# Softmax denominators and row maxima turned by fewer TensorE passes, and new hand-written orders on every engine

## The reference, cut to what matters

```python
x_norm = group_norm(x, gn1_gamma, gn1_beta, GROUPS).reshape(b, c, n)
qkv = jnp.einsum('oc,bcn->bon', qkv_w, x_norm) + qkv_b[None, :, None]
...
attn = jnp.einsum('bhnd,bhmd->bhnm', q, k) / math.sqrt(head_dim)
attn = jax.nn.softmax(attn, axis=-1)
x_attn = jnp.einsum('bhnm,bhmd->bhnd', attn, v)
...
x_attn = jnp.einsum('oc,bcn->bon', out_w, x_attn) + out_b[None, :, None]
x_attn = group_norm(x_attn, gn2_gamma, gn2_beta, GROUPS)
...
x_attn = jax.nn.silu(h1) * gate
x_attn = x_attn @ mlp2_w.T
...
return x + x_attn
```

## Time and profile before

| | us |
|---|---|
| median of 3 runs | 162.49 (162.44 to 163.28) |
| the profiled execution, its own time | 163.85 |
| span of the profiled execution | 162.1 |
| PE busy | 153.3 |
| DVE busy | 100.2 |
| ACT busy | 89.6 |
| POOL busy | 58.0 |

### The profile page before, as it was taken

One profiled execution on the slowest core, in us unless ns is written; L12 is line 12 of the kernel. 1 busy time (PEld: TensorE's weight loads), 2 busy tenths in 40 slices (PEclk: granted clock), 3 DMA queues, 4 the chain that ended last, 5 costly groups with the idle time before them and its releaser, 6 DMA issues.

```text
span 162.1 us, 3214 instructions
## 1 busy us (share of the span) xinstructions
PE 153.3 (95%) x1160; PEld 125.0 (77%) x1160; DVE 100.2 (62%) x223; ACT 89.6 (55%) x160; POOL 58.0 (36%) x107
## 2 busy tenths in 40 slices
PE   7699999999799997999999999999999999999993
PEld 5245786699477776798697999689699698799991
DVE  0750585547999864798487788776947155254331
ACT  8859764523217577576566872345675477424120
POOL 7079985580002075040670000490000671704400
PEclk9999999999999999999999999999999999999999
DMA  3999100424360070600702424100000000001010
GB/s 95 247 395 343 47 4 0 117 77 131 100 165 0 2 194 9 184 11 6 189 8 76 126 70 128 35 2 2 6 0 34 32 4 0 32 0 36 0 65 32
DMA packets 11407, 12.17 MB, mean 75 GB/s; under 512 B 1456, under 2 KB 9584, under 8 KB 11392
## 3 DMA queue, kind: packets, MB, share of 16 engines
q1 hardware_dynamic: 11360, 11.94, 25.3%
q0 software_dynamic: 32, 0.04, 0.3%
HBM read 4.56 MB, written 1.05 MB: 35 GB/s over the span
## 4 chain that ended last, share of the span: by engine, by line
PE 78%; DMA 7%; DVE 6%; SPq 4%; issue 2%; POOL 1%; ACT 1%; DVEq 0%; ACTq 0%; POOLq 0%
PE ps L754 9%; PE po L778 9%; PE pm L728 9%; PE px L849 7%; PE ps L664 5%; SPq L288 4%; PE po L804 4%; PE po L790 3%; PE pm L691 3%; PE pf L664 3%; PE pf L650 3%; DMA k_stack<-qk_parts 3%; PE pf L651 3%; PE pf L652 3%; DVE neg_max L1407 3%; DMA fac<-in_factors 2%
## 5 line engine op out<-in xcount | busy, mean ns | idle before, releaser
L1407 DVE TENSOR_REDUCE neg_max<-pm 128x2 f32<-128x512 f32 x64 | 42.3, 685 | 12.7 <-PE pm L728 12.4
L474 ACT ACTIVATE up_t<-ps 128x512 f32<-128x512 f32 x64 | 36.1, 593 | 16.0 <-PE ps L754 8.6
L728 PE MATMUL pm<-k_stack,q_stack 127*128 127x256 f32 x128 | 28.5, 308 | 2.2 <-DMA k_stack<-qk_parts 1.1
L754 PE MATMUL ps<-q_stack,k_stack 128*128 128x256 f32 x128 | 27.1, 305 | 0.5 <-ACT up_t L474 0.2
L728 PEld LDWEIGHTS pm<-k_stack,q_stack 127*128 127x128 f32 x128 | 19.6, 189 | 7.0 <-issue 2.3
L754 PEld LDWEIGHTS ps<-q_stack,k_stack 128*128 128x128 f32 x128 | 19.4, 189 | 3.5 <-issue 1.2
L359 POOL TENSOR_TENSOR sq<-gs 128x2 f32<-128x2 f32 (+1 forms) x5 | 1.0, 193 | 53.0 <-DVE gs L1362 53.0
L778 PE MATMUL po<-up_t,v_aug 128*32 128x256 f32 x256 | 16.7, 384 | 0.3 <-DVE gs L1362 0.3
L849 PE MATMUL px<-win,w_s 128*128 128x256 f32 x56 | 15.5, 387 | 0.0
L650 PE MATMUL pf<-xm_hi,w_hi 128*128 128x256 f32 x44 | 13.9, 315 | 0.0
L652 PE MATMUL pf<-xm_hi,w_lo 128*128 128x256 f32 x44 | 12.4, 281 | 0.0
(11 more groups left out here) (117 smaller groups left out, 319.3 us busy)
## 6 DMA issues: line engine op xcount, KB each, us to landing
win<-in_xw SPq DMA_DIRECT2D x12, 256.0 KB, 6.7
q_stack<-qk_parts SPq DMA_DIRECT2D x24, 128.0 KB, 2.4
k_stack<-qk_parts SPq DMA_DIRECT2D x24, 128.0 KB, 2.7
out<-win SPq DMA_DIRECT2D x8, 128.0 KB, 1.7
w_s<-in_w SPq DMA_DIRECT2D x1, 512.0 KB, 5.4
w_s<-in_w SPq DMA_DIRECT2D x1, 256.0 KB, 5.9
wqk_s<-in_wqk SPq DMA_DIRECT2D x1, 128.0 KB, 5.5
wo_s<-in_wo SPq DMA_DIRECT2D x1, 128.0 KB, 4.8
```

The costliest lines, as they stand in the source:

```text
L474: act.activation(probs[:, h // HALF, h % HALF, :, :].rearrange("p c n -> p (c n)"), ps[:, h % 2, :], ACT.Exp, scale=D ** -0.5).then_inc(pr ...
L728: return pe.matmul(pm[:, h % 2, c * N:(c + 1) * N], stack_rows(q_stack, i, slice(0, TOP))[:, h, c * 128:(c + 1) * 128], stack_rows(k_stack ...
L754: return pe.matmul(ps[:, h % 2, c * N:(c + 1) * N], stack_rows(k_stack, i, slice(0, TOP + 1))[:, h, c * 128:(c + 1) * 128], stack_rows(q_s ...
L1407: dve.tensor_reduce(neg_max[:, i % 2, :, h], pm[:, h % 2, :].rearrange("p (c n) -> p c n", c=2), AX.X, ALU.max, negate=True).then_inc(max_ ...
```

## The change

`turn_sums` becomes four transposes of whole 128x128 blocks of `sums`, and `invert` reads the 16 denominators of a pixel out of these blocks with a strided pattern. `neg_max` becomes 128 wide for each image, blank but for 16 columns, so that `turn_maxima` is one transpose of a 128x128 tile; ACT reads 16 x 128 in place of 8 x 256, and the DMA of `rows` has 16 pieces for 8. One memset on DVE blanks `neg_max` at the start. And the lists of calls of SP, POOL, ACT, PE and DVE are put in new orders.

```diff
-        neg_max = sb("neg_max", [128, 2, 2, HEADS])
-        max_row = sb("max_row", [HEADS, N], F32R)
+        neg_max = sb("neg_max", [128, 2, 128])
+        max_row = sb("max_row", [2 * HEADS, 128], F32R)
...
-            for j in range(0, 3):
-                stack(j)
+            stack(0)
+            stack(1)
             rows(0)
+            stack(2)
             rows(1)
             stack(3)
...
             stack(5)
+            stack(6)
             rows(4)
-            stack(6)
-            stack(7)
             rows(5)
             store(0)
+            stack(7)
+            store(1)
             rows(6)
             rows(7)
...
-                act.activation(max_row[:, :], pm[0:HEADS, 1, 0:N], ACT.Copy).then_inc(rows_read, 1)
+                act.activation(max_row[:, :], pm[0:2 * HEADS, 1, 0:128], ACT.Copy).then_inc(rows_read, 1)
...
             def turn_maxima(i):
                 pe.wait_ge(max_read, HEADS * (i + 1))
-                for c in range(2):
-                    mm = pe.transpose(pm[0:HEADS, 1, c * 128:(c + 1) * 128], neg_max[:, i % 2, c, :], ident_s[:, :])
-                mm.then_inc(turn_done, 1)
+                if i < 2:
+                    pe.wait_ge(blank_ready, 1)
+                pe.transpose(pm[:, 1, 0:128], neg_max[:, i % 2, :], ident_s[:, :]).then_inc(turn_done, 1)
...
                 for c in range(2):
                     for half in range(2):
-                        a = c * HEADS + half
-                        mm = pe.matmul(po[:, 0, a:a + HEADS - 1:2], sums[:, half, c * 128:(c + 1) * 128],
-                                       ident_s[:, D - D * half::32], start=True, stop=True)
+                        a = (2 * c + half) * 128
+                        mm = pe.transpose(po[:, 0, a:a + 128], sums[:, half, c * 128:(c + 1) * 128], ident_s[:, :])
                 mm.then_inc(den_done, 1)
...
+            dve.memset(neg_max[:, :, :], 0.0).then_inc(blank_ready, 1)
...
-                dve.reciprocal(inv[:, :, :].rearrange("p c h -> p (c h)"), po[:, 0, 0:2 * HEADS]).then_inc(inv_ready, 1)
+                dens = po[:, 0, D:D + 1]
+                dve.reciprocal(inv[:, :, :].rearrange("p c (g u) -> p c u g", u=2),
+                               bass.AP(tensor=dens.tensor, offset=dens.offset, ap=[dens.ap[0], (2 * 128, 2), (128 - D, 2), (32, HALF)])).then_inc(inv_ready, 1)
```

More of the change, by code:

```diff
@@ L887, in _ @@
             maxima(0, 3, 1)
-            downsample(7)
             project_v(1)
@@ L927, in _ @@
+            scores(0, 5, 0)
+            scores(0, 5, 1)
+            maxima(1, 7, 0)
+            maxima(1, 7, 1)
+            weigh(0, 0, 0)
+            weigh(0, 0, 1)
+            scores(0, 6, 0)
+            scores(0, 6, 1)
+            scores(0, 7, 0)
+            scores(0, 7, 1)
             maxima(2, 0, 0)
             maxima(2, 0, 1)
-            scores(0, 4, 0)
-            scores(0, 4, 1)
+            project_qk(3)
             turn_maxima(1)
-            scores(0, 5, 0)
-            scores(0, 5, 1)
@@ L960, in _ @@
             scores(1, 3, 0)
             scores(1, 3, 1)
-            maxima(2, 6, 1)
+            turn_inverse(0)
+            project_qk(4)
             scores(1, 4, 0)
             scores(1, 4, 1)
+            scores(1, 5, 0)
+            scores(1, 5, 1)
             maxima(2, 7, 0)
             maxima(2, 7, 1)
-            turn_sums(0)
-            scores(1, 5, 0)
-            scores(1, 5, 1)
+            maxima(3, 0, 0)
+            project_out(0)
+            turn_maxima(2)
+            maxima(3, 0, 1)
@@ L970, in _ @@
             scores(1, 6, 0)
[L971 removed]
             scores(1, 6, 1)
[L973 to L976 removed]
             scores(1, 7, 0)
             scores(1, 7, 1)
+            project_v(4)
             maxima(3, 1, 0)
             maxima(3, 1, 1)
[L981 to L983 removed]
             maxima(3, 2, 0)
             maxima(3, 2, 1)
[L986 removed]
@@ L993, in _ @@
             weigh(1, 1, 1)
+            project_qk(5)
+            maxima(3, 3, 0)
+            maxima(3, 3, 1)
             maxima(3, 4, 0)
             maxima(3, 4, 1)
-            project_v(4)
+            scores(2, 0, 0)
+            scores(2, 0, 1)
+            scores(2, 1, 0)
+            scores(2, 1, 1)
+            turn_sums(1)
             maxima(3, 5, 0)
@@ L1070, in _ @@
             maxima(5, 2, 1)
-            scores(3, 7, 0)
-            scores(3, 7, 1)
-            project_qk(7)
-            weigh(3, 0, 0)
-            weigh(3, 0, 1)
-            weigh(3, 1, 0)
-            weigh(3, 1, 1)
+            up_project(1, 0, 0)
+            turn_sums(3)
             maxima(5, 3, 0)
             maxima(5, 3, 1)
+            down_project(0, 0)
             maxima(5, 4, 0)
+            maxima(5, 4, 1)
+            down_project(0, 1)
+            turn_inverse(3)
+            maxima(5, 5, 0)
+            maxima(5, 5, 1)
+            up_project(1, 0, 1)
+            maxima(5, 6, 0)
+            maxima(5, 6, 1)
+            up_project(1, 1, 0)
+            project_out(3)
+            maxima(5, 7, 0)
+            maxima(5, 7, 1)
             scores(4, 0, 0)
@@ L1139, in _ @@
+            up_project(3, 1, 1)
             weigh(4, 0, 0)
             weigh(4, 0, 1)
-            maxima(6, 5, 0)
-            maxima(6, 5, 1)
             weigh(4, 1, 0)
+            weigh(4, 1, 1)
+            scores(5, 2, 0)
+            scores(5, 2, 1)
+            down_project(3, 0)
+            scores(5, 3, 0)
+            scores(5, 3, 1)
+            turn_sums(4)
+            down_project(3, 1)
+            scores(5, 4, 0)
+            scores(5, 4, 1)
+            scores(5, 5, 0)
+            scores(5, 5, 1)
@@ L1165, in _ @@
+            weigh(5, 1, 0)
+            weigh(5, 1, 1)
             maxima(7, 1, 0)
+            scores(6, 0, 0)
+            scores(6, 0, 1)
             maxima(7, 1, 1)
@@ L1501, in _ @@
+            reduce_max(2, 0)
             low_parts(3)
-            for j in range(0, 6):
+            for j in range(1, 5):
                 reduce_max(2, j)
-            coefficients(2)
+            invert(0)
             read_v(3)
+            reduce_max(2, 5)
             reduce_max(2, 6)
+            normalise(0)
             reduce_max(2, 7)
-            invert(0)
-            normalise(0)
+            low_parts(4)
             reduce_max(3, 0)
+            statistics(0)
             reduce_max(3, 1)
-            low_parts(4)
```

621 lines of the change are left out of this document (290 added, 331 removed).

## The result

The changed kernel takes 156.23 us in the median of 4 runs (155.28 to 157.64), the kernel before 162.67 us beside it; the ratio is 0.957, with a 95% interval of 0.951 to 0.963. On another occasion, with six more runs, it was 157.14 us and 0.965 (0.960 to 0.970). All ten runs of the changed kernel lie between 155.3 and 158.7 us, with a median of 156.8. The forecast was 156.4, with a range of 154.5 to 159.7.

What follows compares the result with a forecast made beforehand. PE's own work was taken to bound some 110 of 162 us. Savings of 2.8 + 0.9 + 1.6 + 1.0 = 6.3 us, less 0.2 for small waits, took 162.5 to 156.4 us; range 154.5 to 159.7.

Steps and rivals of the forecast that it cites:

- The rival in which DVE becomes the bound: From 45 to 93 us PE's savings turn into waits for `reduce_max`; 2.9 us come back, 159.3 us; chance 0.25.
- Item 1: `turn_sums` on PE: four transposes at 0.44 us replace eight instructions at 0.79; 2.8 us saved over eight images.
- The case in which transposes don't overlap: In `turn_sums`, the four transposes lose 2.4 us instead of gaining 2.8; 161.6 us; chance 0.03.
- Item 2: `turn_maxima` on PE: two transposes at 0.22 us become one at 0.11; 0.9 us saved over eight images.
- Item 3: `weigh` on PE: 14 places become 9 at 0.34 us a place; 1.6 us taken as saved.
- Item 4: PE's 1.1 us wait on a stack DMA before image 3's first `maxima` goes; 1.0 us gained, bounds 0 and 1.3.
- Item 5: SP's list: `rows(0)` ahead of `stack(2)` lets scores begin some 1.9 us earlier; `rows(5)` ahead of `stack(7)`, formerly 2.61 us.
- no wait of PE at image 3: Sign to look for in the chain: PE does not wait on a stack DMA at image 3.
- Item 6: Front: first reduction at about 37.7 us, image 0's turn at 43.8 to 44.0; counted 0, bounds -0.3 to +2.5.
- Item 7: Off the path: `neg_max` memset, strided reciprocal, ACT's smaller copy, `rows` DMA in 16 pieces; all counted 0.
- Item 8: New waits: image 2's `weigh` behind `group_means(3)` 0.5 us, DVE's chain in images 5 and 6 0.3; net 0.
- The case with 0.01: TensorE's clock falls from each image's `turn_sums` to `turn_inverse`, as transposes don't count as activity; 168 us; chance 0.01.

Runs made afterwards that it cites:

- experiment 3: Changed kernel with only `turn_sums` and its reciprocal as before: 160.34 us, ratio 0.986 to the kernel before.
- experiment 4: Changed kernel with `weigh` of images 4, 6 and 7 parted by other calls, six more places: 158.44 us, ratio 0.975 to the kernel before.
- experiment 2: Changed kernel with `turn_sums` and `turn_maxima` as before, so the new orders alone: 160.46 us, ratio 0.986 to the kernel before.
- experiment 9: Changed kernel with `rows(0)` put behind `stack(2)` in SP's list: 163.19 us, ratio 1.001 to the kernel before.
- experiment 10: Changed kernel with `rows(5)` put behind `stack(7)` in SP's list: 163.6 us, ratio 1.006 to the kernel before.
- experiment 1: Kernel before with the new `turn_sums` and `turn_maxima`, all old orders kept: 162.18 us, ratio 0.995 to the kernel before.
- experiment 11: Kernel before with both new operations and, in SP's list alone, `rows(0)` ahead of `stack(2)`, `rows(5)` ahead of `stack(7)`: 161.91 us, ratio 0.989.
- experiment 6: Changed kernel with 12 unread constant products in PE's idle places between the maxima of images 0 and 1: 156.16 us, ratio 0.962.
- experiment 8: Changed kernel with SP's whole list of calls as before: 170.98 us, ratio 1.052 to the kernel before.
- experiment 5: Changed kernel itself, unaltered, timed again in six more runs: 157.14 us, ratio 0.965 to the kernel before.
- experiment 7: Kernel before with 11 unread constant products in PE's idle places of the same early stage: 162.49 us, ratio 1.000.
- experiment 12: Changed kernel with 12 constant products, and ACT issuing two of six stack DMAs of images 1 and 2: 157.35 us, ratio 0.966.

## Why the prediction was right, and where it was not

*The bound.* Right in the main: PE's own work bounds the run behind 73 us, and what was taken out of it there shortened the run by its full amount (experiments 3 and 4). Ahead of that the chain goes through DVE for 7 us. The rival in which DVE becomes the bound is refuted all the same: PE waited 0.2 us for `reduce_max` and 0.3 for the group means.

*Item 1, `turn_sums`.* The mechanism was right (four transposes overlap: 0.44 us, 0.273 each), the size a quarter too small: 0.47 us an image and 3.7 in all where 2.8 stood (experiment 3). The case in which transposes don't overlap is ruled out.

*Item 2, `turn_maxima`.* One instruction fewer for each image, as counted. Apart from item 1 it was not measured finely enough: experiments 2 and 3, which differ by it, are at 160.46 and 160.34 us, where 0.9 was counted. So this term is not shown.

*Item 3, places of `weigh`.* 0.34 us a place was counted and 0.33 measured (experiment 4): 1.6 us for five.

*Item 4, the stack wait.* This term was wrong. Image 3's wait shrank from 1.1 us to 0.2, but images 1 and 2 now wait for theirs. Image 1's stack starts later by the front's new order. Image 2's does not start later because of SP's list, as item 5 feared: its `project_qk` now stands on PE behind the wait for image 1's stack, at 42.86 us (44.5 with the 1.6 us by which this profile's front was quicker), where it was at 41.20, and SP's issues follow ACT's copy of it. The waits add up to 1.3 us, so the 1.0 was not gained. The prediction's sign for this term, no wait of PE at image 3, failed, and PE was held for `stack(2)` at 50.9 us, by 0.4.

*Item 5, SP's order.* "No gain by itself, and none lost" (at the end of item 6) hid what this move does. In the new order of PE the two moved rows are worth 6.4 to 6.8 us each (experiments 9 and 10); the item had at most 1.9 and 2.6 us in view. It asked what the move gives in the old order of PE, where 4.9 us of work stood between image 0's turn and its scores (43.78 to 48.65). In the new one it is 2.7 us (42.57 to 45.26), and `stack(2)` begins later than the row is ready. It did not enter the sum, for both kernels that were compared have the row where their PE needs it.

*Item 6, the front.* Right within 0.3 us. With these 1.6 us added, the first reduction starts at 38.0 us (37.7 forecast), image 0's maxima are turned at 44.2 (43.8 to 44.0) and its first scores begin at 46.9 (47.0). The last six of its reductions follow without a gap as counted, in DVE's timeline, and PE's shows the scores:

```profile
38.52 3.87 DVE L1411 TENSOR_REDUCE neg_max<-pm 128x2 f32<-128x512 f32 x6
```

```profile
45.26 0.52 PE L758 MATMUL ps<-q_stack,k_stack 128*128 128x256 f32 x3
```

*Item 7.* The reciprocal with its strided read takes 255 ns on the mean, as before (0.26), and ACT's copy of the maxima 0.27 instead of 0.37. Little of it was on the path: the chain has one copy (0.28 us) and 0.14 us of one reciprocal.

*Item 8.* Image 2's `weigh` waits 0.3 us for the group means, as one did before, where 0.5 was counted. This is where the chain comes out of DVE.

*The sum.* 6.1 us were forecast, 5.7 to 7.0 measured. That the number came out so near is in part luck. Item 1 was 0.9 us too small and item 4's 1.0 us did not come, which nearly cancel; item 2's 0.9 is not shown, and the clock, counted at nothing, took some of what came (7.0 us at full clock, and seven of ten executions were below it). The forecast's own range, 154.8 to 158.0, doesn't follow from the bounds named beside it: items 3 and 4 at their lower bounds alone give 158.3, and with item 8 doubled 159.1. What the terms left out besides is that they don't add up independently: new operations and new orders are worth 0.8 and 2.3 us by themselves, and some 3 us come only when both are there. In the old orders the time that PE saves ends at a row of maxima that has not landed (1.5 and 1.0 us, experiment 1), and if the row comes sooner, at stacks and reductions (experiment 11). These are waits of one profile each; that they are the whole of the 3 us is not shown.

*The clock.* The case with 0.01 had a true effect and the wrong cause. Nothing ties the clock to transposes: the changed kernel has 56 of them for 32, and experiment 6 with the same 56 held the clock in all six executions, while experiment 2 with the old 32 lost it in three of six. But in eight of the experiments' profiles the granted clock stood at half from some point between 42 and 50 us, for 3.4 to 10 us. The changed kernel took 155.3 to 155.5 us at full clock, 155.7 to 157.6 at a mean of 0.989 and 157.6 to 158.7 at 0.978, so the fall costs up to three microseconds. The prediction counted on a clock that stays up, because the one profile of before showed it so.

## What to carry to other kernels

When every engine runs a fixed list, price a moved DMA against the consumer's list as it will be, not as it is: count what the consumer has left to do before it, and when the DMAs ahead of it in the queue can start. If the consumer has nothing left, the whole queue ahead of the DMA is on the path. An operation made cheaper on the bounding engine may return its saving only when all lists are fitted to it again (here 0.8 us of 3.7 without that); test the operation and the order apart before crediting either. Where single runs spread by 3 us, compare those at the same granted clock. And before moving issues to a second queue, see whether the wait is for the issues or for the transfers themselves.

## What the runs showed of the hardware

- The granted clock fell to half in the middle of kernels, in the stage that DVE paces, with no single wait of PE over 1 us ahead of it in experiments 2 to 4. It fell in the profiles of experiments 1 to 4 and 8 to 11, and again at PE's long waits for a row in experiments 8 and 10. It did not in those of before, of the changed kernel (experiment 5 too) and of experiments 6, 7 and 12.
- Constant products in PE's idle places keep it up. With them all 12 executions of the changed kernel (experiments 6 and 12) and all 12 of the kernel before (experiment 7) have a mean granted clock of 0.998 or more; without them 3 of 10 of the changed kernel, and 14 of 17 of the kernel before beside experiment 7. What exactly the clock answers to is not shown.
- The first upsampling instructions stand at 1.98 us for four in some profiles and at up to 3.78 in others, also among kernels with one list for PE (experiments 10 and 9), while the granted clock reads 1.00 in both. It moves the first `downsample` by 1.6 us.
- Going from products in groups of 32 columns to ordinary ones and back costs 0.33 us each time (experiment 4).
- An fp32 transpose of 128x128 costs 0.11 us in a row of them though one lasts 0.27. An fp32 product with only 4 moving columns stands as two instructions and costs 0.10 us for each. The weight load of the same 128x128 block lasts 0.14 us for the transpose and 0.19 for each instruction of the product.
- Six DMAs of 128 KB between SBUF partitions were not quickened by a second queue in experiment 12: the last one took 4.50 us to land instead of 2.49.
